# Shorter quantisation and top-2, and a Mamba state's two channel halves scanned in one instruction of 1024

## The reference

```python
x = x + 0.5 * fp6_linear(layernorm(x))       # blocks of 32 quantised to an FP6 grid, weights too
x = x + causal_attention(layernorm(x))       # one head
x = x + 0.5 * fp6_linear(layernorm(x))
x = x + 0.5 * switch_head(layernorm(x))      # 16 heads, 8 experts, top 2 for values and for outputs
x = x + mamba(layernorm(x))                  # 256 channels, 16 states, sequence 512
x = x + 0.5 * switch_head(layernorm(x))

def mx_quantize(blocks):                     # of 32
    scales = max(max(abs(blocks)) / 7.5, 1e-30)
    q = nearest_on_fp6_e2m3_grid(blocks / scales)   # ties to the lower value

def switch_head(x):
    w, sel = top_k(gate_v, 2)                # per token and head, over the experts
    mix_v = sum(sigmoid(w) * one_hot(sel))   # multiplies the experts' values
    ...                                      # softmax attention in each head
    mask_o = one_hot(top_k(gate_o, 2)).sum() # selects the experts' output matrices

def mamba_step(h, dt, B, C, x):              # h: 256 channels x 16 states
    h = exp(dt * A) * h + (dt * x) * B
    y = sum(h * C, over the states)
```

## Time and profile before

| | |
|---|---|
| median of 3 runs | 2786.88 us |
| lowest, highest | 2774.88, 2787.03 us |
| the profiled execution | 2787.38 us |
| its span | 2785.5 us |
| mean granted TensorE clock | 0.965 of full speed |

### The profile page before, as it was taken

How to read it: one execution, slowest core, us unless ns; L and a number is a source line. 1 busy time by engine, 2 the same in 40 slices (tenths; PEclk the granted TensorE clock), 3 DMA queues, 4 the chain that set the end, 5 groups by cost and what they waited for, 6 DMA issues and landing times.

```text
span 2785.5 us, 51284 instructions
## 1 busy us (share of the span) xinstructions
PE 2584.8 (93%) x17437; PEld 1716.1 (62%) x17437; DVE 2181.1 (78%) x3233; ACT 1853.1 (67%) x4430; POOL 737.0 (26%) x564
## 2 busy tenths in 40 slices
PE   4699999989999999999899999999999999999997
PEld 3566675665666756666565666656566665666665
DVE  7588786989799798988987888797788868775552
ACT  3265755857687676866766767686677768666563
POOL 1000000434145124603540343164145315410000
PEclk9699999999999999999999999999999999999998
DMA  3425354564565546555563654556466564545423
GB/s 135 114 85 132 93 147 100 140 183 112 148 156 161 137 124 178 136 136 152 145 165 103 169 155 137 149 167 176 112 172 169 132 164 141 167 122 147 108 80 91
DMA packets 753407, 385.77 MB, mean 138 GB/s; under 512 B 421568, under 2 KB 678656, under 8 KB 752768
## 3 DMA queue, kind: packets, MB, share of 16 engines
q1 hardware_dynamic: 747104, 380.66, 50.7%
q10 hardware_dynamic: 6048, 1.84, 0.3%
HBM read 274.91 MB, written 115.87 MB: 140 GB/s over the span
## 4 chain that ended last, share of the span: by engine, by line
PE 62%; DVE 21%; issue 9%; ACT 3%; DMA 2%; POOL 2%; SPq 1%; ACTq 0%; DVEq 0%; POOLq 0%
PE ps L723 13%; PE ps L732 11%; PE ps L745 11%; PE ps L792 8%; PE ps L712 6%; DVE h_ring L1234 6%; PE ps L798 4%; DVE h_nmax L1054 3%; PE ps L805 2%; DVE h_ring L1244 2%; PE ps L764 1%; POOL h_ring L659 1%; PE ps L832 1%; ACT h_prob L899 1%; DVE h_wide_a L1206 1%
## 5 line engine op out<-in xcount | busy, mean ns | idle before, releaser
L899 ACT ACTIVATE h_prob<-ps,h_nmax 128x512 f32<-128x512 f32 x1024 | 710.0, 695 | 134.6 <-DVE h_nmax L1054 132.7
L1054 DVE TENSOR_REDUCE h_nmax<-ps 128x2 f32<-128x1024 f32 x512 | 621.3, 1213 | 147.4 <-PE ps L723 147.1
L732 PE MATMUL ps<-ident,h_prob 128*128 128x128 f32 x4096 | 623.1, 279 | 26.3 <-DVE h_probT L1295 13.5
L732 PEld LDWEIGHTS ps<-ident,h_prob 128*128 128x128 f32 x4096 | 480.7, 144 | 197.0 <-issue 118.5
L723 PE MATMUL ps<-h_qk 64*128 64x512 f32 x2048 | 592.1, 655 | 0.5 <-ACT h_prob L899 0.3
L668 POOL TENSOR_TENSOR h_wide_c<-h_wide_c,h_ring 128x512 f32<-128x512 f32 x240 | 331.3, 1381 | 734.3 <-DVE h_ring L1244 734.3
L1019 ACT ACTIVATE h_probT<-ps 128x512 f32<-128x512 f32 x796 | 478.5, 601 | 61.6 <-PE ps L732 59.2
L745 PE MATMUL ps<-h_probT,h_v_sb 128*64 128x256 f32 x4096 | 504.0, 389 | 5.4 <-DMA h_v_sb<-v_d 3.2
L745 PEld LDWEIGHTS ps<-h_probT,h_v_sb 128*64 128x64 f32 x4096 | 273.8, 138 | 314.0 <-issue 147.0
L1234 DVE TENSOR_TENSOR_SCAN h_ring<-h_ring 128x512 f32<-128x512 f32 x256 | 395.1, 1543 | 36.2 <-POOL h_ring L659 20.2
L659 POOL TENSOR_TENSOR h_ring<-h_m_xpad,h_m_b_rows 128x512 f32<-128x512 f32 x256 | 348.9, 1373 | 257.5 <-DVE h_m_xpad L1354 250.1
(11 more groups left out here) (222 smaller groups left out, 2669.3 us busy)
## 6 DMA issues: line engine op xcount, KB each, us to landing
h_mix_diag<-mix_blocks SPq DMA_DIRECT2D x128, 512.0 KB, 3.8
v_d<-h_v_mixed SPq DMA_DIRECT2D x128, 256.0 KB, 4.2
h_v_sb<-v_d SPq DMA_DIRECT2D x128, 256.0 KB, 3.3
at_d<-h_att SPq DMA_DIRECT2D x128, 256.0 KB, 2.9
h_mo_diag<-mo_blocks SPq DMA_DIRECT2D x128, 256.0 KB, 3.5
h_att<-at_d SPq DMA_DIRECT2D x128, 256.0 KB, 3.7
h_m_b_rows<-dbl_d SPq DMA_DIRECT2D x128, 256.0 KB, 4.3
h_m_c_rows<-dbl_d SPq DMA_DIRECT2D x128, 256.0 KB, 4.3
```

The source lines that it names most:

```text
L732: ins = pe.transpose(ps[:, TB + v % 2, k * P:(k + 1) * P], prob[:, v % NB, k * P:(k + 1) * P], ident[:, :])
L899: act.activation(prob[:, v % NB, :], ps[:, SB + v % 4, :], ACT.Exp, bias=nmax[:, p, j, o:o + 1], accum_out=den[:, p, j, o:o + 1]).then_inc ...
L1054: dve.tensor_reduce(nmax[:, p, j, :], ps[:, SB + 2 * w % 4:SB + 2 * w % 4 + 2, :], X, ALU.max, negate=True).then_inc(sem("row_max"), 1)
```

## The change

It touches three things.

*Quantisation, 15 parts to 12 (13 instructions).* The grid step is held as its inverse: the exponent bits are turned over by a second bit operation in part 4, so multiplication scales `z` to whole numbers, and adding and subtracting one constant (1.5 * 2^23) rounds. A second bit operation in part 7 turns the exponent back. The clamp at 7.5 is gone.

*Top-2, 7 parts to 6.* The first choice is written where it is kept, without a copy. `mix_gates` computes `(tanh + 1) * choice` in one instruction for each tile; the factor 0.5 of the sigmoid goes into the value weights `Wve`. `MIX_AT` and the steps of the two stores behind top-2 follow `TOP_PARTS` and come two steps earlier.

*Scan of 1024.* A unit is now a state. Drive, scan, read and add take both halves in one instruction; the decay stays two instructions of ACT (512 and 511 elements), and the first decay of the second half is zero, set once by POOL, so that the scan starts anew there. The ring has two places of 1024 for drives and states and two for decays: the same memory. `SCAN_AT` has 16 entries, four or five steps apart; `add` of a state stands in the step of its read, and the next `drive` one step ahead of the next scan.

```diff
-        QUANT_PARTS = 15
+        QUANT_PARTS = 12
...
-                link(dve.tensor_scalar(p2.bitcast(U32), z.bitcast(U32), 0x7F800000, None, ALU.bitwise_and))
+                link(dve.tensor_scalar(p2.bitcast(U32), z.bitcast(U32), 0x7F800000, 0x7F800000, ALU.bitwise_and, ALU.bitwise_xor))
             elif i == 5:
-                link(dve.tensor_scalar(p2, p2, 1.0, 4.0, ALU.max, ALU.min))
+                link(dve.tensor_scalar(p2, p2, 0.5, 2.0, ALU.max, ALU.min))
             elif i == 6:
-                link(dve.tensor_scalar(mg, p2, ROUND, None, ALU.mult))
+                link(dve.scalar_tensor_tensor(out=mg, in0=z, scalar=4.0, in1=p2, op0=ALU.mult, op1=ALU.mult))
             elif i == 7:
-                link(dve.tensor_tensor(t, z, mg, ALU.add))
+                link(dve.tensor_scalar(p2.bitcast(U32), p2.bitcast(U32), 0x7F800000, None, ALU.bitwise_xor))
+                link(dve.tensor_scalar(t, mg, ROUND, ROUND, ALU.add, ALU.subtract))
             elif i == 8:
-                link(dve.tensor_tensor(t, t, mg, ALU.subtract))
-
+                link(dve.tensor_tensor(mg, t, mg, ALU.subtract))
             elif i == 9:
-                link(dve.tensor_tensor(mg, t, z, ALU.subtract))
+                link(dve.scalar_tensor_tensor(out=t, in0=mg, scalar=0.5, in1=t, op0=ALU.is_ge, op1=ALU.subtract))
             elif i == 10:
-                link(dve.scalar_tensor_tensor(out=mg, in0=mg, scalar=16.0, in1=p2, op0=ALU.mult, op1=ALU.is_ge))
-            elif i == 11:
-                link(dve.scalar_tensor_tensor(out=mg, in0=mg, scalar=0.125, in1=p2, op0=ALU.mult, op1=ALU.mult))
-            elif i == 12:
-                link(dve.tensor_tensor(t, t, mg, ALU.subtract))
-            elif i == 13:
-                link(dve.tensor_scalar(t, t, -FP6_MAX, FP6_MAX, ALU.max, ALU.min))
+                link(dve.scalar_tensor_tensor(out=t, in0=t, scalar=-0.125, in1=p2, op0=ALU.mult, op1=ALU.mult))
...
-        TOP_PARTS = 7
-        UN = NS * HALVES
-        NSC, NDC = 5, 3
+        TOP_PARTS = 6
+        NSC, NDC = 2, 2
...
-        SCAN_AT = [23 + v * 70 // UN for v in range(UN)]
+        SCAN_AT = [23 + v * 70 // NS for v in range(NS)]
...
+                        if n == 0:
                             pool.wait_ge(sem("dtx"), b + 1)
+                            if b == 0:
+                                pool.memset(mb["decay"][:, :, S:S + 1], 0.0).then_inc(sem("decay_zero"), 1)
                         pool.wait_ge(sem(f"b_in{n % 2}"), 16 * (NS // 2 * b + n // 2 + 1))
-                        wait_place_free(pool, b, v)
-                        pool.tensor_tensor(mb["scan"][:, (b * UN + v) % NSC, :], mb["xpad"][:, h, CONV - 1:],
-                                           mb["b_rows"][:, n % 2, :], ALU.mult).then_inc(sem("drive"), 1)
...
+                        wait_place_free(pool, b, n)
+                        pool.tensor_tensor(by_half(mb["scan"][:, (b * NS + n) % NSC, :]), mb["xpad"][:, :, CONV - 1:],
+                                           both(mb["b_rows"][:, n % 2, :]), ALU.mult).then_inc(sem("drive"), 1)
...
+                        pool.tensor_tensor(mb["y"], mb["y"], by_half(mb["scan"][:, (b * NS + n) % NSC, :]),
                                            ALU.add).then_inc(sem("summed"), 1)
...
-                        act.activation(mb["decay"][:, w % NDC, :], mb["th"][:, h, :], ACT.Exp,
-                                       scale=A_neg[:, h, n:n + 1]).then_inc(sem("decay"), 1)
+                        for h in range(HALVES):
+                            to = mb["decay"][:, w % NDC, h * S + (h > 0):(h + 1) * S]
+                            ins = act.activation(to, mb["th"][:, h, (h > 0):], ACT.Exp, scale=A_neg[:, h, n:n + 1])
+                        ins.then_inc(sem("decay"), 1)
...
-                    act.activation(Wve_split[:, 0, :], WveT, ACT.Copy).then_inc(sem("Wve_hi"), 1)
+                    act.activation(Wve_split[:, 0, :], WveT, ACT.Copy, scale=0.5).then_inc(sem("Wve_hi"), 1)
...
-                        elif part == 5 and r == 0:
-                            if a == 1 and i >= 1:
+                            if r == 0 and a == 1 and i >= 1:
                                 dve.wait_ge(sem("mo_out"), 16 * i)
-                            link(dve.tensor_copy(pick, key))
-                        elif part == 5:
+                            link(dve.tensor_tensor(pick if r == 0 else key, key, top, ALU.is_equal))
+                        elif r == 1:
                             dve.tensor_tensor(pick, pick, key, ALU.add).then_inc(sem("chosen"), 1)
...
-                        link(dve.tensor_scalar(g_sig[:, :, :], g_sig[:, :, :], 0.5, 0.5, ALU.mult, ALU.add))
...
-                            ins = dve.tensor_tensor(mix[:, j, :, :].rearrange("p e h -> p h e"),
-                                                    g_sig[:, j, :].rearrange("p (h e) -> p h e", e=E),
-                                                    chosen[:, 0, j, :].rearrange("p (h e) -> p h e", e=E), ALU.mult)
+                            ins = dve.scalar_tensor_tensor(out=mix[:, j, :, :].rearrange("p e h -> p h e"),
+                                                           in0=g_sig[:, j, :].rearrange("p (h e) -> p h e", e=E), scalar=1.0,
+                                                           in1=chosen[:, 0, j, :].rearrange("p (h e) -> p h e", e=E),
+                                                           op0=ALU.add, op1=ALU.mult)
...
-                                if u == SCAN_AT[-1] + 3:
+                                if u == SCAN_AT[-1] + 4:
                                     gate_y(n)
```

More of the change, by code:

```diff
@@ L310, in wait_taken, with wait_place_free @@
             eng.wait_ge(sem("extra_free_dve" if what in BY_DVE else "extra_free"), taken[what, c, n])
[L313 to L318, removed]
+        def wait_place_free(eng, b, n):
+            if b * NS + n >= NSC:
+                b_, n_ = divmod(b * NS + n - NSC, NS)
+                if n_ == 0:
+                    eng.wait_ge(sem("read"), b_ * NS + 1)
                 else:
[L320 removed]
+                    eng.wait_ge(sem("summed"), b_ * (NS - 1) + n_)
         dbl_d = nc.dram_tensor("dbl_d", (2 * NS, S), F32).ap()
@@ L354, in macaron_kernel @@
             SB, TB, EB = 0, 4, 6
-            ring = t("ring", [P, (NSC + NDC) * S])
+            ring = t("ring", [P, (NSC + NDC) * HALVES * S])
             wide_a = t("wide_a", [P, 4 * S])
@@ L364, in split, with by_half, both @@
                 return a.rearrange("p (n s) -> p n s", n=n)
+            def by_half(a):
+                return a.rearrange("p (h s) -> p h s", h=HALVES)
+            def both(row):
+                return row.rearrange("p (a s) -> p a s", a=1).broadcast_to([P, HALVES, S])
             def blocks(a):
@@ L373, in macaron_kernel @@
             TRI = J * (J + 1) // 2 * P
-            mb = {"scan": split(ring[:, 0:NSC * S], NSC), "decay": split(ring[:, NSC * S:(NSC + NDC) * S], NDC),
+            mb = {"scan": split(ring[:, 0:NSC * HALVES * S], NSC),
+                  "decay": split(ring[:, NSC * HALVES * S:(NSC + NDC) * HALVES * S], NDC),
                   "conv": split(wide_a[:, 0:2 * S], HALVES), "th": split(wide_a[:, 2 * S:4 * S], HALVES),
@@ L696, in _ @@
                                     layer_norm_power(pool, "m_ln", mb, n)
-                                for v in range(UN):
+                                for v in range(NS):
                                     if u == SCAN_AT[v] - 1:
                                         drive(n, v)
-                                for v in range(HALVES, UN):
+                                for v in range(1, NS):
                                     if u == SCAN_AT[v] + 1:
@@ L1227, in step_size, with scan @@
                         dve.tensor_scalar(dt, dt, 1e-4, None, ALU.max).then_inc(sem("dt"), 1)
-                    def scan(b, v):
-                        w = b * UN + v
+                    def scan(b, n):
+                        w = b * NS + n
+                        if w == 0:
+                            dve.wait_ge(sem("decay_zero"), 1)
                         dve.wait_ge(sem("decay"), w + 1)
@@ L1262, in _ @@
                         if 5 <= g < 8:
-                            for i in range(5 * (g - 5), 5 * (g - 4)):
+                            for i in range(QUANT_PARTS // 3 * (g - 5), QUANT_PARTS // 3 * (g - 4)):
                                 quantise_part(dve, link, linked, w_raw["L0_w"].rearrange("p a (n b) -> p (a n) b", b=QBLOCK),
@@ L1323, in _ @@
                             elif kind == "mamba":
-                                for v_ in range(UN):
+                                for v_ in range(NS):
                                     if u == SCAN_AT[v_] + 1:
```

53 lines of the change are left out of this document (23 added, 30 removed).

## The result

The changed kernel takes 2766.18 us (median of 6 runs, 2761.14 to 2771.55), against 2786.56 us for the kernel before (6 runs): ratio 0.9938, 95% interval 0.9914 to 0.9961. That is 20 us; 39 were forecast. The profiled execution has a span of 2766.3 us.

What follows compares the result with a forecast made beforehand. PE, 93% busy in the scan stages, was taken to limit what returns. 54 us of DVE there x 0.64 = 35, plus 12 outside, less 8 for the ring, gave 39 us: 2787 - 39 = 2748 us, range 2715 to 2773.

Steps and rivals of the forecast that it cites:

- The fused scan: DVE's scans and reads, 256 of 512 each becoming 128 of 1024: saves 33 us of DVE, from 0 to 40.
- Rival 2: Scan stages: gain not seen, DVE's time returns as idle behind 3.5 us lumps, row maxima late; 2780 us, chance 0.19.
- The new serial chain: Scan, read, add, next drive form a ring over two places: 24 us of waits expected, 8 us reaching the end.
- Rival 4: The scan, read, add, drive ring takes 11.23 us or more and sets every state's pace: 2831 us, chance 0.08.
- Top-2: Copies L1127 and L1138 go: 24 us of DVE, 13 in scan stages; earlier mix and mo stores taken as nothing.
- The price 0.64: Scan stages: each us of DVE time estimated worth 0.64 us of length, from comparing two sorts of stage.
- Blocks: DVE and POOL excluding each other: 96 us on scans and reads moves to other instructions, the two effects cancelling.
- Rivals 1 and 3: DVE-POOL blocks: 1, they vanish, 2718 us, chance 0.2; 3, they grow to 294 us, 2836 us, chance 0.1.

Runs made afterwards that it cites:

- par_even: Changed kernel with every scan in a step that has a row maximum ahead of it, scans four or six steps apart: 2758.44 us, 0.9886 to the kernel before.
- par_odd: Changed kernel with every scan in a step without a row maximum, so that one follows at once: 2804.31 us, 1.0053 to the kernel before.
- q_only: Kernel before with the new quantisation, top-2, mix_gates and value weights, scans still 512 wide: 2721.32 us, 0.9774 to the kernel before.
- pair_half: `q_only` with its scans of 512 in pairs at the changed kernel's 16 steps, four places and four decays: 2753.67 us, 0.9876 to the kernel before.
- q_late: `q_only` with mix_gates and the two stores moved back to the steps of the kernel before: 2762.5 us, 0.9904 to the kernel before.
- pool_halves: Changed kernel with POOL's drive and add each cut into two instructions of 512: 2762.76 us, 0.9907 to the kernel before.

## Why the prediction was wrong

Its direction was right and its amount twice too high, and both for a reason that it did not have: two large errors of opposite sign nearly cancelled. The fused scan was forecast as a gain of 13 us and is a loss of 46 to 57; the rest was forecast as a gain of 25 us and is one of 63. That their sum has the forecast sign is luck.

- *The fused scan*, forecast as 33 us of DVE x 0.64 less 8 for the ring, a gain of 13 us. This is the step that failed. Its instruction lengths held (2300 and 1216 ns measured, 2290 and 1230 forecast), but alone the fused scan costs 57 us. The sum priced every us off DVE alike, wherever it stood, and lacked what stands behind the instruction in DVE's queue. One scan of 2.3 us holds the next row maximum back, and ACT waits. That such placement matters is shown: `par_even` and `par_odd` lie 46 us apart, and a read right behind the scan costs 20. How much of the loss it is, is shown only in part: the better placement took 15 us off the changed kernel, and the fused scan is then still 1.1% (31 us) above `q_only`. Some 28 us come with pairs of old scans at every fourth or fifth step (`pair_half`), by a way that stays open. Rival 2 named the lump and took a gain of zero for it; it is a loss.
- *The new serial chain.* Its idle time came (43.2 us put down to POOL, 24 forecast). Its price of 8 us is neither shown nor excluded: with that wait gone the time fell by 0.2% (6 us), within the noise, while blocks on the scans came back. Rival 4 is out: it took over 100 us of such waits.
- *Top-2.* "nothing in the steady part waits for them" was wrong of the stores. The two steps are worth 36 us; SP waited at the mix store and at the load behind it in every job, which a look at the waits of SP's own queue would have shown. This is the second step that failed, a term put at nothing. The instructions taken away, quantisation and top-2 together, gave 27 us (`q_late`) for 44 us of DVE work (2181.1 to 2137.0), 0.61; forecast were 25.
- *The price 0.64.* It came from stages that differ in the kind of work too. Removing work and leaving the order as it is gives 0.33 to 0.61, removing it by wider instructions gives less than nothing.
- *Blocks.* That they move from scans to the other instructions was right, and in the whole change they nearly cancel: DVE's total fell by 78 us against 79. For the fused scan by itself they don't (18 us off DVE against 33). The page "SBUF — State Buffer" of the Trainium skill, section "Who interferes with whom", says that a DVE instruction with two SBUF inputs contends with a GpSimd instruction that reads SBUF. The trace agrees (L1129, with two such inputs, takes 1032 ns instead of 716). What the time of the blocks costs is not shown by itself: `pool_halves` shortened them and stood 0.3% below the changed kernel, with intervals that overlap, but with longer waits ahead of scans. Rivals 1 and 3 fell by DVE's busy time: 2103 us is neither near 2000 nor above 2181.

What stays open: the 31 us by which `par_even` stands above `q_only`, where no row maximum stands right behind a scan; how the 17 us of width divide between DVE's and POOL's instructions; and how the earlier mix acts beyond the 19 us seen at L792. `par_even` and `par_odd` have spacings of four and six steps and not of four and five; against each other this doesn't matter, against the changed kernel it might.

## What to carry to other kernels

Where engines hand small pieces to each other at a steady beat, price an edit by what it puts ahead of the piece on the beat, not by the busy time that it takes off: fusing the instructions of a state's two halves took 0.14 us off DVE (18 us in 128 states) and cost 0.45 us (57 in 128). When an edit shortens a chain whose length sets a timetable, cost the moved steps by themselves, and read the waits of the DMA queue and of the engine that uses the data for them. Time the parts of a change apart: a small net result can hide a gain of 2% that needs only one half of it.

## What was not expected of the hardware

The same 128 scans, reads, drives and adds of the same widths took 46 us more or less in total by one step's difference in place. In the lengths of single instructions little was unexpected: a scan of 1024 took 2300 ns against 2 x 1.21 us for two of 512. POOL's add of 1024 took 2394 ns on average, less than an undisturbed 2 x 1.25 us, where blocks had been expected to stretch it to 2.8 us.
